# A two-layer cross-attention and expert kernel: half steps from a table, shorter ends, and key blocks summed on GpSimd

## The reference, cut to what matters

```
x = x + attention_A(layernorm(x), ctx, ctx, key mask) @ W.T + b        # kind A: masked softmax
x = x + ternary(layernorm(x))                    # Hadamard, round to 4 bits, ternary weights
x = x + block(layernorm(x), ctx, bias)           # attention with bias (kind C), gelu network, two layernorms
x = x + experts(layernorm(x))                    # 8 experts, each takes its 512 best tokens
```

## Time and profile before

| | |
|---|---|
| median of three runs | 1060.68 us |
| profiled execution, its span | 1055.02 us, 1052.9 us |
| first instruction to last logits | 788.2 us |
| routing and experts | 264.7 us |
| TensorE busy | 877.3 us (83%) |
| VectorE busy | 653.2 us (62%) |
| ScalarE busy | 382.3 us (36%) |
| GpSimd busy | 282.6 us (27%) |
| chain that ended last, by engine | PE 63%, DVE 20%, issue 6%, ACT 5%, POOL 3%, DMA 2% |

### The profile page before, as it was taken

One profiled execution on the slowest core, in us unless ns is written; L12 is line 12 of the kernel. 1 busy time (PEld: TensorE's weight loads), 2 busy tenths in 40 slices (PEclk: granted clock), 3 DMA queues, 4 the chain that ended last, 5 costly groups with the idle time before them and its releaser, 6 DMA issues.

```text
span 1052.9 us, 18932 instructions
## 1 busy us (share of the span) xinstructions
PE 877.3 (83%) x7691; PEld 628.8 (60%) x7691; DVE 653.2 (62%) x1500; ACT 382.3 (36%) x589; POOL 282.6 (27%) x260
## 2 busy tenths in 40 slices
PE   4999777889988989999898887877742289999995
PEld 3566554455665665665665664555632269998985
DVE  3445387686588588688678588274217746666442
ACT  0313133234424423523622613223110066666772
POOL 3200212012014014013112003011222238877752
PEclk8899899989999999999999999879875579999998
DMA  8211443433333442442432336130004024455541
GB/s 291 91 31 36 180 161 126 151 119 122 132 135 108 152 152 87 165 157 89 148 120 110 116 145 231 40 121 21 20 22 158 15 66 121 120 142 148 137 75 21
DMA packets 47700, 120.63 MB, mean 115 GB/s; under 512 B 4737, under 2 KB 33921, under 8 KB 39425
## 3 DMA queue, kind: packets, MB, share of 16 engines
q1 hardware_dynamic: 41472, 111.06, 30.8%
q0 software_dynamic: 6144, 8.39, 4.4%
HBM read 111.05 MB, written 8.39 MB: 113 GB/s over the span
## 4 chain that ended last, share of the span: by engine, by line
PE 63%; DVE 20%; issue 6%; ACT 5%; POOL 3%; DMA 2%; SPq 0%; POOLq 0%; DVEq 0%; ACTq 0%
PE ps_v L411 12%; PE row_scores L335 10%; PE row_scores L1183 5%; PE ps_m L428 4%; PE ps_v L1200 3%; PE ps_r L1200 3%; DVE probs L592 3%; PE ps_r L386 2%; PE ps_m L420 2%; DVE row_max L562 2%; PE ps_v L420 2%; PE key_scores L355 2%; DVE row_scores L569 2%; PE ps_m L305 2%; PE ps_m L312 2%
## 5 line engine op out<-in xcount | busy, mean ns | idle before, releaser
L746 ACT ACTIVATE probs<-probs 128x1024 f32<-128x1024 f32 x64 | 67.6, 1057 | 263.3 <-DVE probs L592 263.2
L569 DVE CUSTOM_DVE_ANT_0 row_scores<-row_scores,bias_q 128x256 f32<-128x256 f32 x256 | 100.9, 456 | 62.0 <-PE row_scores L335 61.7
L743 ACT ACTIVATE probs<-key_scores 128x1024 f32<-128x1024 f32 x64 | 65.5, 1023 | 156.2 <-PE key_scores L351 156.2
L562 DVE TENSOR_REDUCE row_max<-row_scores 128x4 f32<-128x1024 f32 x64 | 78.1, 1220 | 66.4 <-PE row_scores L335 66.4
L335 PE MATMUL row_scores<-k_op_c,q_op_C 32*128 32x256 f32 x512 | 77.0, 419 | 17.1 <-DVE q_op_C L578 16.2
L335 PE MATMUL row_scores<-k_op_a,q_op_A 32*128 32x256 f32 x512 | 79.9, 432 | 8.1 <-DVE q_op_C L578 8.1
L592 DVE TENSOR_TENSOR probs<-key_scores,bias_k 128x1024 f32<-128x1024 f32 x64 | 77.9, 1217 | 7.5 <-PE key_scores L351 7.3
L351 PE MATMUL key_scores<-q_op_C,k_op_c 32*128 32x256 f32 x512 | 79.6, 431 | 0.1
L351 PE MATMUL key_scores<-q_op_A,k_op_a 32*128 32x256 f32 x512 | 74.6, 410 | 0.9 <-DVE q_op_A L578 0.9
L335 PEld LDWEIGHTS row_scores<-k_op_c,q_op_C 32*128 32x128 f32 x512 | 46.4, 193 | 44.9 <-issue 31.2
L335 PEld LDWEIGHTS row_scores<-k_op_a,q_op_A 32*128 32x128 f32 x512 | 48.4, 200 | 39.2 <-issue 24.6
(11 more groups left out here) (226 smaller groups left out, 2131.1 us busy)
## 6 DMA issues: line engine op xcount, KB each, us to landing
bias_q<-in_bias_q SPq DMA_DIRECT2D x32, 1024.0 KB, 4.9
bias_k<-in_bias_k SPq DMA_DIRECT2D x32, 1024.0 KB, 4.9
w1e<-in_w1e SPq DMA_DIRECT2D x8, 1024.0 KB, 4.9
w2e<-in_w2e SPq DMA_DIRECT2D x8, 1024.0 KB, 6.8
k_op_a<-in_k_a SPq DMA_DIRECT2D x32, 128.0 KB, 2.3
mask_int<-in_mask SPq DMA_DIRECT2D x8, 512.0 KB, 5.7
v_op_A<-in_v_a SPq DMA_DIRECT2D x8, 512.0 KB, 5.2
w<-in_w SPq DMA_DIRECT2D x2, 1024.0 KB, 8.6
```

Of the source, the lines that this page charges most:

```text
L562: nc.vector.tensor_reduce(of, row_scores[:, :, :].rearrange("p j (t k) -> p j t k", t=QT), AX_X, ALU.max).then_inc(max_taken, 1)
L569: ins = nc.vector.tensor_tensor_reduce(row_scores[:, j, qt * SEQ:(qt + 1) * SEQ], row_scores[:, j, qt * SEQ:(qt + 1) * SEQ], bias_q[:, m % ...
L743: nc.scalar.activation(of, key_scores[:, :, :], ACT.Exp).then_inc(exp_done, 1)
L746: nc.scalar.activation(of, of, ACT.Exp).then_inc(exp_done, 1)
```

## The change

**Positions.** A of batch 0 moves to positions -4 to -1, next to batch 1. C of batch 7 moves to 62 to 65, one position after batch 6.

**A table.** `PE_SLOT`, `VE_SLOT`, `AC_SLOT` and `PO_SLOT` give each side job its half step; `move()` gives batches 0, 1 and 4 to 7 steps of their own. Each side function is now called by job name. Banks are handed on by a computed order (`TURN`), and T_F and f1 of batch 7 use score banks. In the middle f1's second piece moves from half step 10 to 11, w_v from 3 to 6, the layer norm of A two half steps ahead, and f2 becomes eight pieces of two products in half steps 0 (two), 2, 3 (three), 5 and 6. The last logits move from half step 172 to 146.

**Scores apart.** Where the present and the next quad are of one kind, `pe_scores_apart` writes all of `row_scores` ahead of `key_scores`.

**Key blocks.** GpSimd adds block 1 of `probs` to block 0 after each exponential, 128 additions of 128x2x256. The product with ones then takes block 0 alone: 8 products in place of 16 per chunk. So that the values stay right, GpSimd subtracts the values of block 0 from those of block 1 (16 times). The values now wait for GpSimd's sum in place of the exponential. Of the output's affine step one of GpSimd's three operations moves to half step 12, ahead of it.

```diff
-            grid[8 * (b - 1) + (w if b < 2 else 2 * w)] = Quad(A, b, w)
-            grid[8 * (b + 1) + (1 + w if b > NB - 3 else 1 + 2 * w)] = Quad(C, b, w)
+            grid[8 * (b - 1) + (w + 4 if b == 0 else w if b == 1 else 2 * w)] = Quad(A, b, w)
+            grid[8 * (b + 1) + (w - 2 if b == 7 else 1 + w if b == 6 else 1 + 2 * w)] = Quad(C, b, w)
...
+PE_SLOT = {"wb": -6, "wa": 2, "T_A": -32, "T_B": 4, "wo": 36, "had": 5, "wv": 22, "T_F": 39, "T_q": 7, "tern": 8, "f1_0": 40,
...
+           "f2_0": 48, "f2_1": 48, "f2_2": 50, "f2_3": 51, "f2_4": 51, "f2_5": 51, "f2_6": 53, "f2_7": 54}
...
+move(0, T_q=6, qT=6, qcap=5, tern=7, yq=7, x2=7, wk=8, kC=8, stC=8, rsC=8, apC=9, T_C=10, xcT=10, wq=11, qC=11,
...
+def due(slots, step):
+    return [(job, b) for job in slots for b in (BATCHES if job != "wb" else [0]) if step_of(slots, job, b) == step]
...
+        def pe_scores_apart(pe, now, then, half):
+            pe_wait_maximum(pe, then, half)
...
+            for t in range(QT):
+                for j in heads_of(group(then, half)):
+                    ins_then = pe_maximum_scores(then, j, t)
+            ins_then.then_inc(max_scores, 1)
+            pe_wait_scores(pe, now, half)
...
+            pe.wait_ge(max_added, half_number(now, half) + 1)
+            for t in range(QT):
+                for j in heads_of(group(now, half)):
+                    ins_now = pe_scores(now, j, t)
...
-            pe.wait_ge(exp_done, 2 * last + 2)
...
+            pe.wait_ge(blocks_summed, 2 * last + 2)
+            pe.wait_ge(v_parted[q.kind], q.b + 1)
+            bank_free(pe, "values", (q.kind, q.b, q.c))
             for what in ("values", "sums"):
                 col = 0 if what == "values" else SEQ
                 for par in range(2):
-                    for kb in range(QT):
+                    for kb in range(QT if what == "values" else 1):
...
+        def pe_f2(pe, f, t, part, last):
+            pe.wait_ge(S["gelu_done"], 4 * f + part + 1)
+            for hc in (2 * part, 2 * part + 1):
...
+        def po_sum_blocks(po, q, half):
+            n = number(q)
+            po.wait_ge(exp_done, 2 * n + half + 1)
+            both = probs[:, n % 4, heads(q, half), :, :]
+            nc.gpsimd.tensor_tensor(both[:, :, 0, :], both[:, :, 0, :], both[:, :, 1, :], ALU.add).then_inc(blocks_summed, 1)
...
+            nc.gpsimd.tensor_tensor(v[:, :, 1, :], v[:, :, 1, :], v[:, :, 0, :], ALU.subtract).then_inc(v_parted[kind], 1)
...
+        def po_previous(po, step):
+            pos, half = divmod(step - 1, 2)
+            q = quad_of(pos)
+            if q is not None:
+                po_sum_blocks(po, q, half)
+                if q.w == 1 and half == 0:
+                    po_part_values(po, q.kind, q.b)
```

More of the change, by code:

```diff
@@ new lines, with move @@
+MOVED = {}
+def move(b, **steps):
+    for job, step in steps.items():
+        MOVED[job, b] = step
+move(0, T_q=6, qT=6, qcap=5, tern=7, yq=7, x2=7, wk=8, kC=8, stC=8, rsC=8, apC=9, T_C=10, xcT=10, wq=11, qC=11,
+     stA=-32, rsA=-32, apA=-31, xb=-31, T_A=-30, qA=-30, wv=19, vC=19)
+move(1, stA=-9, rsA=-9, apA=-8, xb=-8, T_A=-7, qA=-7, mk=-10)
+move(4, f2_2=111, f2_3=111, f2_4=112, f2_5=112, f2_6=113, f2_7=113, f2_0=111, f2_1=111, yf=113, rsG=113, apG=114, aff=114,
+     stR=116, rsR=116, apR=117, T_R=122, xrT=122, lg=123, lgc=123)
@@ new lines, with bank_name, turns @@
+OTHER_BANK = {("T_F", 7): "k0", ("f1_0", 7): "k1", ("f1_2", 7): "r0", ("f1_3", 7): "r1"}
+def bank_name(job, b):
+    if job == "values":
+        return "v"
+    return OTHER_BANK.get((job, b), PE_BANK[job][0])
+def turns():
+    names = list(PE_SLOT)
+    found = {}
+    for bank in ("m0", "m1", "v"):
+        jobs = [(step_of(PE_SLOT, job, b), names.index(job), job, b) for job in PE_BANK
+                for b in (BATCHES if job != "wb" else [0]) if bank_name(job, b) == bank]
+        if bank == "m1":
+            jobs += [(step_of(PE_SLOT, "wb", 0), names.index("wb"), "wb", 0)]
+        if bank == "v":
+            jobs += [(values_step(*k), -1, "values", k) for k in CHUNKS]
+        jobs.sort(key=lambda j: j[:2])
+        for (_, _, job, b), (_, _, then, at) in zip(jobs, jobs[1:]):
+            if job == "values":
+                found[then, at] = ("norm_done", CHUNK_NO[b] + 1)
+            else:
+                _, name, each, first = PE_BANK[job]
+                found[then, at] = (name, each * b + first)
+    return found
@@ L93, in wait @@
+TURN = turns()
 def wait(eng, sem, value):
@@ L540, in pe_layers @@
                 maximised, of_half = previous_half(step)
-                if now is not None or then is not None:
+                if now is not None and then is not None and now.kind == then.kind:
+                    pe_scores_apart(pe, now, then, half)
+                elif now is not None or then is not None:
                     pe_round(pe, now, then, half)
@@ L546, in pe_layers @@
                     pe_values(pe, past)
-                pe_side(pe, *divmod(step, 16))
-                if step == -11:
+                for job, b in due(PE_SLOT, step):
+                    pe_side(pe, job, b)
+                if step == -5:
                     pe.wait_ge(S["wb_copied"], 2)
-                if step in (-16, -15, -14) or -11 <= step <= 14:
+                if -10 <= step <= 16 and step not in (-6,):
                     pe_keep_busy(10)
@@ new lines, in ve_side @@
+            if job == "apG":
+                wait(ve, S["x3_ready"], b)
+                wait(ve, S["hb_T"], ahead(VE_SLOT, "apB", "apG", b))
+                ve_ln_apply(ve, "G", b, nrm["G"], lambda t: y_attn[b % 2][:, t, :])
+            if job == "stR":
+                ve.wait_ge(S["x3_ready"], b + 1)
+                ve_ln_stats(ve, "R", b, xtile(b))
+            if job == "apR":
+                wait(ve, S["xr_T"], b)
+                wait(ve, S["stored_n"], 16 * b)
+                ve_ln_apply(ve, "R", b, nrm["R"], xtile(b))
@@ L730, in ve_layers @@
                     ve_add_maximum(ve, maximised, of_half)
-                ve_side(ve, *divmod(step, 16))
+                for job, b in due(VE_SLOT, step):
+                    ve_side(ve, job, b)
                 if half == 1 and past is not None and past.par == 1:
@@ L883, in po_layers @@
         def po_layers(po):
-            for pos in range(FIRST, LAST):
-                i, k = divmod(pos, 8)
-                po_side(po, i, 2 * k)
-                po_side(po, i, 2 * k + 1)
+            for step in range(2 * FIRST, 2 * LAST):
+                po_previous(po, step)
+                for job, b in due(PO_SLOT, step):
+                    po_side(po, job, b)
         def ve_constants(ve):
```

495 lines of the change are left out of this document (239 added, 256 removed), and 4 rows, old and new, of the table PE_BANK.

## The result

The changed kernel took 1024.35 us (median of four executions, 1022.71 to 1037.9) against 1060.39 us beside it. The ratio is 0.9687, its 95% interval 0.9605 to 0.977. That is faster, by 36.0 us between medians, where 53.7 were forecast. The profiled execution took 1025.06 us, 30.0 us less than the one of before. One execution of the run with filler products, at 1038.52 us, was in a slower state and is left out of that run's median.

What follows compares the result with a forecast made beforehand. TensorE was taken to bound the middle, a chain of waits the end. Start 5, first period 4, middle 18.9 and end 26 made 54 us off 1055.0, 1001; with 5.7 for the median, 1007 (996 to 1017).

Steps and rivals of the forecast that it cites:

- the sum: Whole kernel: 54 us off the profiled execution's 1055.0, plus 5.7 for the median of the runs: 1006.7, said as 1007.
- Part 1: Products with ones in the middle: halving them takes 3.8 us of TensorE per batch.
- part 2: Side jobs spread over half steps in the middle; with the halved products, 4.4 us less per batch.
- Part 3: GpSimd's sums: 1.27 to 1.67 us each, slowed norms cost 0.4 us per batch; net middle gain 18.9 us.
- The rival built on it: VectorE blocked by GpSimd's sums in seven pairs per batch: 10 us per batch slower, 1089 us; chance 0.03.
- Part 4: Start: A of batch 0 beside batch 1, A half steps about 4.0 us, C's first scores about 5 us earlier.
- the chain: Start, Hadamard product to the queries of C: 30 us before, some 19 needed by its own links.
- Part 5: End: C of batch 7 begins after 75 us, shorter half steps of C alone, 26 us gained (bounds 12 and 36).
- Behind the last values: End, from the last division through f1 and f2 to the logits: 43.5 us with queueing, in place of 58.85.
- the middle gives nothing: Rival: TensorE's savings in the middle turn into waiting for VectorE, only the ends pay: 1026 us; chance 0.22.
- GpSimd as the bound: Rival: sums as long as the mask's 3.65 us make GpSimd set the middle's pace, 1066 us; chance 0.05.

Runs made afterwards that it cites:

- the paired run: Changed kernel with row scores and key scores of neighbouring quads of one kind interleaved again instead of one after the other: 1018.39 us, ratio 0.9593.

## Why the prediction was right in its direction and wrong in a third of its size

In the profiled executions the change is 30.0 us where 54 were forecast. Between medians it is 36.0 of 53.7: the profiled execution of before was 5.7 us below its median, as the sum says, but that of the changed kernel lies 0.7 above its own. By stage, from starts and ends of the windows of both traces: the start 2.4 (forecast 5), the first period 3.8 (4), the middle up to the last values of A 17.4 (18.9), the end 5.9 (26).

- **Part 1 and part 2, the middle: right, by two errors that cancel.** The period fell by 3.7 to the forecast 4.0. But halving the products is worth 2.5 of its 3.8 us, the table 2.5 to 3.3 where 0.6 was left for it (4.4 - 3.8), and the sums cost 1.9 where 0.4 stood. That the total came out is luck.
- **Part 3, the sums: duration right, side effect mis-sized.** 1.27 us each, and no values wait for one in the middle. What they cost beside that, priced at 0.4 us per batch on the ground of the earlier trace rows, is 1.9; 0.9 of it is norm F, by the run with the quantisation first, and the rest was not taken apart. The reading of the earlier trace rows failed: that norm begins 0.05 us ahead of the mask, not inside it. Another mask and norm of the same trace:

```profile
336.61 3.65 POOL L839 TENSOR_SCALAR mask_bf<-mask_int 128x1024 bf16<-128x1024 int32 x1
...
339.15 1.25 DVE L618 TENSOR_SCALAR nrm_C<-x_all,mv_C,rstd_C 128x256 f32<-128x256 f32 x1
```

This norm begins inside the mask and ends at 340.40, 0.15 us after it; three more of that trace do so. Beside the sums the pair ended 0.15 us after GpSimd's second operation. The rule from the Trainium skill (SBUF — State Buffer, section "Who interferes with whom"), that such operations of VectorE and GpSimd exclude each other, agrees with these rows, and "slowed, not blocked" was read off a norm that began first. It does not hold for norms that begin in the middle of a mask, which keep their length (last section). The rival built on it was still far off with 10 us per batch: two pairs of norms meet the sums in a steady period, not seven, and each waits for one or two operations.
- **Part 4, the start.** The half step of 4.02 us was right, and w_q begins 5.1 us earlier (115.89 against 121.03), as the chain had it. C's first scores, two rounds of A later, come 2.4 us earlier, half of the forecast. Both gains are no larger than chance: the first Hadamard product lies at 95.72 us here and at up to 100.87 in runs with the same start. Filler included, TensorE has no idle time in such a half step; so the serial pairs, not the chain, held the start, as the paired run shows by its 9.5 us.
- **Part 5, the end: the step that failed.** "The half steps of C alone fall from 4.60 to about VectorE's own 3.4 plus side jobs." They did not fall: from the half step at 599.33, now at 575.72, C of batch 7 begins after 82.9 us (forecast 75, before 81.3), and the last values end after 133.5, where 119 were forecast and 130 stood before. The earlier trace rows shows one short half step; before, the additions of C of batches 6 and 7 stood 5.4 and 5.3 us apart on average, and they now stand 7.0 and 6.1 apart. From the first addition of batch 6 to the last of batch 7, before (the changed kernel's line stands with the paired run, 590.55:696.95):

```profile
610.70:717.01 106.31, 83.96 (x689) 58.33 (x678) 72.33 (x210) 28.80 (x44) 18.13 (x23) 0.89 0.34 127
```

It was 106.31 us and is 106.40. The pause between the two batches fell from 31.3 us to 15.2, as the change meant it to, and the half steps grew by as much. The work in this stretch stayed: VectorE is busy for 75.2 us (72.3 before), 4.7 for each of the sixteen half steps, and TensorE for 91.0 (84.0 before, 82.4 with paired scores), 5.7 for each. The step took VectorE's loop, named the side jobs without adding them up, and never summed TensorE's work: in the 133.5 us TensorE is busy for 116.7 (72.89 + 43.79), nearly the 119 that were forecast for all of it. And the cover is poor. In some half steps TensorE waits for VectorE's maximum (4.3 us in all), for the gelu (4.1) or the load of the context (1.2), in others VectorE for TensorE's row scores (15.2). Neither the clock nor the order of the scores nor VectorE's jobs alone changed the stretch; the jobs and the load together took 3.35 us off. What the other 11 of the missing 14.5 would need stays open.
- **Behind the last values** 43.5 us were forecast (the terms named make 39.1, and no row shows the 4.4 of queueing) and 49.4 measured. That term's chain began with the division, but the table has f2 and y of batch 6 ahead of it; moving them gave 6.4 us. This was in the order of the instructions, and could have been read there.

The measured 1024 lies outside the forecast's own 996 to 1017. Of the rivals, "the middle gives nothing" stands at 1026, next to it, but its mechanism did not happen: the middle gave what the forecast said, and the end did not. GpSimd as the bound is refuted by its busy share of 49% in the middle.

## What to carry to other kernels

A stretch in which several engines take turns as the bound is priced by the sum of each engine's work over it, and then by what queues in one half step; an engine's own loop is only a floor. Taking out a pause shortens nothing by itself where the work that stood in it moves into the half steps beside it. Work moved to an idle engine is not free because that engine is idle: look at what runs beside it. An edit that gains nothing may be hidden by the next wait a few microseconds on: look for where its lead was lost before dropping it.
